# A mixture-of-experts stage on one Trainium2 core: W1 as the stationary operand, fetched for every tile of tokens

## The reference, cut to what matters

```python
def _L1_ffn_ref(x, router_W, router_b, ln_g, ln_b, W1, b1, W2, b2):
    B, S, H, E, K = (2, 512, 256, 8, 2)          # x here is 2 x 2048 x 256
    logits = x @ router_W + router_b
    w, idx = jax.lax.top_k(logits, K)
    w = jax.nn.softmax(w, axis=-1)
    gates = jnp.einsum('bske,bsk->bse', jax.nn.one_hot(idx, E, dtype=x.dtype), w)
    ...
    h = xhat[:, :, None, :] * ln_g + ln_b        # xhat: x, normalized
    a = jax.nn.gelu(jnp.einsum('bseh,ehf->bsef', h, W1) + b1, approximate=False)
    y = jnp.einsum('bsef,efh->bseh', a, W2) + b2
    y = y + x[:, :, None, :]
    out = jnp.einsum('bseh,bse->bsh', y, gates)
    return out
```

## Time and profile before

| | us |
|---|---|
| median of 3 runs | 4070.68 |
| lowest and highest | 4062.64, 4073.54 |
| the profiled execution, its own time | 4065.74 |
| its span in the trace | 4064.2 |
| PE busy in the span | 3197.6 (79%) |
| DVE busy | 2557.4 (63%) |
| ACT busy | 1755.8 (43%) |
| POOL busy | 1472.8 (36%) |

### The profile page before, as it was taken

How to read it: one execution, slowest core, us unless ns; L and a number is a source line. 1 busy time by engine, 2 the same in 40 slices (tenths; PEclk the granted TensorE clock), 3 DMA queues, 4 the chain that set the end, 5 groups by cost and what they waited for, 6 DMA issues and landing times. The chain is left out here.

```text
span 4064.2 us, 72075 instructions
## 1 busy us (share of the span) xinstructions
PE 3197.6 (79%) x21589; PEld 1637.2 (40%) x21590; DVE 2557.4 (63%) x6592; ACT 1755.8 (43%) x2093; POOL 1472.8 (36%) x811
## 2 busy tenths in 40 slices
PE   5539999999999989998335887788887339999970
PEld 2202333333333333332123454455565216666650
DVE  6739998989898989991476777354444302222226
ACT  3302887878787878889211222111211102222210
POOL 2212777777777777778100000000000230000016
PEclk8756999999999999999667999899997569999985
DMA  4743333333333333330230000110001550000014
GB/s 112 216 113 75 82 84 81 75 82 76 81 76 80 77 80 77 79 62 26 50 61 16 11 15 0 71 41 29 25 22 78 206 201 31 31 31 31 31 47 143
DMA packets 200466, 285.30 MB, mean 70 GB/s; under 512 B 91760, under 2 KB 156272, under 8 KB 197840
## 3 DMA queue, kind: packets, MB, share of 16 engines
q1 hardware_dynamic: 185968, 234.81, 23.0%
q0 software_dynamic: 13312, 43.30, 3.0%
q10 hardware_dynamic: 864, 3.15, 0.2%
HBM read 185.37 MB, written 79.00 MB: 65 GB/s over the span
## 5 line engine op out<-in xcount | busy, mean ns | idle before, releaser
L690 DVE CUSTOM_DVE_ANT_0 ps_r<-ps_r,toep 128x512 f32<-128x512 f32 x2048 | 1356.2, 717 | 194.8 <-PE ps_r L623 137.6
L779 ACT ACTIVATE prob<-ps_s,csc 128x1024 f32<-128x1024 f32 x768 | 836.7, 1119 | 185.1 <-PE ps_s L645 134.6
L623 PE MATMUL ps_r<-p 96*128 96x512 bf16 x2048 | 746.4, 403 | 130.9 <-DMA p<-scr_scratch 78.7
L737 POOL TENSOR_TENSOR tb<-tb,toep 128x1024 f32<-128x1024 f32 x256 | 606.1, 2367 | 484.7 <-ACT tb L769 336.6
L645 PE MATMUL ps_s<-p 120*128 120x512 bf16 (+1 forms) x2048 | 618.2, 384 | 41.9 <-ACT tb L769 26.6
L740 POOL TENSOR_TENSOR tb<-tb,mb 128x1024 f32<-128x1024 f32 x256 | 605.6, 2366 | 20.1
L661 PE MATMUL ps_o<-prob,vp 128*32 128x256 f32 x8192 | 553.1, 388 | 1.0 <-ACT prob L779 1.0
L623 PEld LDWEIGHTS ps_r<-p 96*128 96x128 bf16 x2048 | 199.1, 98 | 601.5 <-DVE mp L690 323.8
L769 ACT ACTIVATE tb<-ps_s 128x1024 f32<-128x1024 f32 x256 | 263.0, 1027 | 202.2 <-PE ps_s L645 202.1
L661 PEld LDWEIGHTS ps_o<-prob,vp 128*32 128x32 f32 x8192 | 214.8, 109 | 280.1 <-issue 190.7
L645 PEld LDWEIGHTS ps_s<-p 120*128 120x128 bf16 (+1 forms) x2048 | 181.6, 99 | 273.2 <-ACT prob L779 70.5
(11 more groups left out here) (289 smaller groups left out, 3540.2 us busy)
## 6 DMA issues: line engine op xcount, KB each, us to landing
p<-scr_scratch SPq DMA_DIRECT2D x288, 192.0 KB
mb<-mrow_scratch SPq DMA_DIRECT2D x16, 2048.0 KB, 7.1
scr_scratch<-part SPq DMA_DIRECT2D x64, 384.0 KB, 6.1
moe_w<-in_W_dram SPq DMA_DIRECT2D x16, 1024.0 KB
p<-scr_scratch SPq DMA_DIRECT2D x96, 128.0 KB
slots_scratch<-l_zero POOLq DMA_DIRECT2D x16, 592.0 KB, 5.2
e_xs<-slots_scratch SPq DMA_DIRECT2D x74, 128.0 KB, 2.0
yslots_scratch<-e_y SPq DMA_DIRECT2D x72, 128.0 KB, 1.7
```

What stands on the lines that cost most here:

```text
L623: pe.matmul(ps_r[:, bank, :], buf[:, hh, 0, qt * P:(qt + 1) * P], buf[:, hh, 1, kc * CH:(kc + 1) * CH], start=True, stop=True)\
L690: dve.tensor_tensor_reduce(ps_r[:, bank, :], ps_r[:, bank, :], toep[:, col:col + CH], 1.0, -3.0e38, ALU.mult, ALU.max, mp[:, whose.par, hh ...
L737: pool.tensor_tensor(tb[:, k % DIAGS], tb[:, k % DIAGS], toep[:, col:col + CH].unsqueeze(1) .broadcast_to([P, 2, CH]), ALU.mult).then_inc( ...
L779: act.activation(prob[:, n % RING], ps_s[:, mine % 2], ACT.Exp, scale=csc[:, qb * TB + kb:qb * TB + kb + 1]).then_inc(s["exp"], 1)
```

## The change

- The product of `up` is turned round. W1's 128 x 128 pieces are the stationary operand and `hT` (128 tokens) is the moving one: 16 products with 128 columns. The result has the hidden units on the partitions, which is the layout that `down` needs, so the 8 transposes, `ps_t` and ACT's copies are gone, and the gelu writes `aT` directly. `aT` has two buffers now.
- W1 isn't kept for all experts any more. SBUF holds it for two tiles; `stage_scatter` loads those of the first two, and in `stage_experts` SP's queue fetches the 1 MB of the tile after next once `up` of `this` has read its buffer. SP reads the expert from `owner` for that.
- Tokens: four buffers instead of two, loaded four tiles ahead. The loops have 18 passes with four tiles each.
- Results are stored from ACT's queue, behind the gelu of the next tile.
- b1, ln_g and ln_b are loaded as 96 rows of 128 and turned once by PE in `stage_scatter` into `cols`, a column for each row. The bias of a hidden unit is then a value per partition and piece, read with a stride of zero along the tokens. b2 and W2 stay as they were.
- The tables that go with it grow from 74 to 76 tiles (`AHEAD`), and two stages have more semaphores: 11 instead of 8, and 16 instead of 14.

The diff, cut:

```diff
-AHEAD = 2
+AHEAD = 4
+XS = 4
...
+COLS = E * (FK + 2 * KC)
...
 def stage_scatter(nc, g, a, w):
-        s = open_block(nc, ctx, "w load0 load1 put0 put1 ready eps passed", "s_")
+        s = open_block(nc, ctx, "w turn cols ident load0 load1 put0 put1 ready eps passed", "s_")
...
+        rows = sb("rows", [COLS, P])
...
+                sp.dma_start(rows[0:E * FK, :], a["b1"].rearrange("e (c p) -> (e c) p", p=P)).then_inc(s["w"], 16)
+                for i, n in enumerate(("ln_g", "ln_b")):
+                    at = E * FK + i * E * KC
+                    sp.dma_start(rows[at:at + E * KC, :], a[n].rearrange("e (c p) -> (e c) p", p=P)).then_inc(s["w"], 16)
+                for par in range(2):
+                    e = sp.value_load(g["owner"][0:1, par:par + 1], min_val=0, max_val=E - 1)
+                    sp.dma_start(w["w1"][:, par].unsqueeze(1), a["W1"][bass.ds(e, 1)].rearrange("a (c p) f -> p a c f", p=P))\
+                      .then_inc(s["w"], 16)
                 for e in range(E):
-                    sp.dma_start(w["w1"][:, e], a["W1"][e].rearrange("(c p) f -> p c f", p=P)).then_inc(s["w"], 16)
                     sp.dma_start(w["w2"][:, e], a["W2"][e].rearrange("(c p) n -> p c n", p=P)).then_inc(s["w"], 16)
-                    for n in ("ln_g", "ln_b"):
-                        sp.dma_start(w[n][:, e], a[n][e].rearrange("(c p) -> p c", p=P),
-                                     allow_slow_non_contiguous=True).then_inc(s["w"], 16)
...
+                    sp.dma_start(w["b2"][:, e], a["b2"][e].partition_broadcast(P)).then_inc(s["w"], 16)
...
+            @block.tensor
+            def _(pe):
+                pe.wait_ge(s["w"], up_to(16 * (5 + 2 * E)))
+                pe.transpose(ps_c[:, 0:COLS], rows[:], g["ident"][0:COLS, 0:COLS]).then_inc(s["turn"], 1)
...
 def stage_experts(nc, g, a, w):
...
-        xs = sb("xs", [P, 2, D])
+        xs = sb("xs", [P, XS, D])
...
-        u = sb("u", [P, 2, FF])
-        h = sb("h", [P, 2, FF])
-        aT = sb("aT", [P, FK, P])
+        u = sb("u", [P, 2, FK, P])
+        aT = sb("aT", [P, 2, FK, P])
...
             def _(sp):
...
                 def body(this, one, two):
-                    load(two)
-                    hold(sp, s["y"], this.times(1, 1), s["passed"])
-                    sp.dma_start(g["yslots"][bass.ds(this.times(P), P), :], y[:, this.par]).then_inc(s[f"store{this.par}"], 16)
+                    e = expert(sp, two)
+
+                    hold(sp, s["up"], this.times(1, 1), s["passed"])
+                    fetch(Tile(this.n, this.c + XS))
+                    sp.dma_start(w1[:, this.par].unsqueeze(1), a["W1"][bass.ds(e, 1)].rearrange("a (c p) f -> p a c f", p=P))\
+                      .then_inc(s[f"wfill{this.par}"], 16)
...
                 def up(tile):
-                    e = expert(pe, tile)
                     pe.wait_ge(s["affine"], up_to(tile.times(KC, KC)))
+                    if not isinstance(tile.n, int):
+                        pe.wait_ge(s[f"wfill{tile.par}"], up_to(tile.half(16)))
...
-                    for kc in range(KC):
-                        for half in range(2):
-                            mm = pe.matmul(ps_u[:, tile.par, half * CH:(half + 1) * CH], hT[:, kc, :],
-                                           w["w1"][:, bass.ds(e, 1), kc, half * CH:(half + 1) * CH]
...
+                    for f in range(FK):
+                        for kc in range(KC):
+                            mm = pe.matmul(ps_u[:, tile.par, f, :], w1[:, tile.par, kc, f * P:(f + 1) * P], hT[:, kc, :],
+                                           start=(kc == 0), stop=(kc == KC - 1), skip_group_check=True)
...
                 def body(this, one, two):
                     up(one)
-                    for half in range(2):
-                        if half == 0:
-                            pe.wait_ge(s["act"], up_to(this.times(1, UP0 + 1)))
-
-                        pe.wait_ge(s["trev"], up_to(this.times(2, half - 1 + FREE0)))
-                        for j in range(HALF):
-                            f = half * HALF + j
-                            mm = pe.transpose(ps_t[:, half, j * P:(j + 1) * P], h[:, this.par, f * P:(f + 1) * P], ident[:])
-                        mm.then_inc(s["tr"], 1)
                     turn(two)
                     e = expert(pe, this)
                     pe.wait_ge(s["y"], up_to(this.times(1)))
+                    pe.wait_ge(s["act"], up_to(this.times(1, UP0 + 1)))
...
             @block.scalar
...
-                    act.wait_ge(s["tr"], up_to(tile.times(2, FREE0 - 2)))
-                    act.activation(h[:, tile.par], u[:, tile.par], ACT.Gelu).then_inc(s["act"], 1)
+                    act.wait_ge(s["down"], up_to(tile.times(1, UP0 - 1)))
+                    act.activation(aT[:, tile.par], u[:, tile.par], ACT.Gelu).then_inc(s["act"], 1)
...
                     gelu(one)
+                    hold(act, s["y"], this.times(1, 1), s["passed"])
+                    act.dma_start(g["yslots"][bass.ds(this.times(P), P), :], y[:, this.par]).then_inc(s[f"kept{this.par}"], 16)
...
-                    dve.tensor_tensor(u[:, tile.par], ps_u[:, tile.par], of(w["b1"], e), ALU.add).then_inc(s["biased"], 1)
+                    dve.tensor_tensor(u[:, tile.par], ps_u[:, tile.par], of(b1, e).unsqueeze(2).broadcast_to([P, FK, P]),
+                                      ALU.add).then_inc(s["biased"], 1)
```

More of the change, by code:

```diff
@@ L1936, in walk @@
             start()
-            with eng.Fori(0, SLOT_TILES // 2) as n:
-                for c in range(2):
+            with eng.Fori(0, SLOT_TILES // XS) as n:
+                for c in range(XS):
                     body(Tile(n, c), Tile(n, c + 1), Tile(n, c + 2))
@@ L1943, in _ @@
             def _(pool):
[L1944 to L1947, removed]
+                pool.memset(aT[0:1, 0, 0, 0:1], 0.0).then_inc(s["biased"], UP0)
+                pool.memset(aT[0:1, 0, 0, 1:2], 0.0).then_inc(s["act"], UP0)
+                pool.memset(aT[0:1, 0, 0, 2:3], 0.0).then_inc(s["down"], UP0)
         with nc.Block() as block:
@@ L1951, in _, with fetch @@
             def _(sp):
[L1952 to L1956, removed]
+                def fetch(tile):
+                    sp.dma_start(xs[:, tile.c % XS], g["slots"][bass.ds(tile.times(P), P), :])\
+                      .then_inc(s[f"fetched{tile.c % XS}"], 16)
                 def body(this, one, two):
-                    load(two)
-                    hold(sp, s["y"], this.times(1, 1), s["passed"])
-                    sp.dma_start(g["yslots"][bass.ds(this.times(P), P), :], y[:, this.par]).then_inc(s[f"store{this.par}"], 16)
-                walk(sp, lambda: [load(Tile(0, c)) for c in range(2)], body)
+                    e = expert(sp, two)
[3 more added lines that the diff above has]
+                      .then_inc(s[f"wfill{this.par}"], 16)
+                walk(sp, lambda: [fetch(Tile(0, c)) for c in range(XS)], body)
                 for par in range(2):
-                    sp.wait_ge(s[f"store{par}"], up_to(16 * SLOT_TILES // 2))
-                    sp.wait_ge(s[f"load{par}"], 16 * (SLOT_TILES // 2 + 1))
+                    sp.wait_ge(s[f"wfill{par}"], up_to(16 * (SLOT_TILES // 2)))
+                for i in range(XS):
+                    sp.wait_ge(s[f"fetched{i}"], up_to(16 * (SLOT_TILES // XS + 1)))
             @block.tensor
@@ L1970, in turn @@
                 def turn(tile):
-                    pe.wait_ge(s[f"load{tile.par}"], tile.half(16) + 16)
+                    pe.wait_ge(s[f"fetched{tile.c % XS}"], up_to(tile.quarter(16, 16)))
                     if not (isinstance(tile.n, int) and tile.c == 0):
@@ L2069, in body @@
                     e = expert(dve, this)
-                    dve.wait_ge(s["down"], up_to(this.times(1, 1)))
-                    dve.wait_ge(s[f"store{this.par}"], up_to(this.half(16)))
+                    dve.wait_ge(s["down"], up_to(this.times(1, UP0 + 1)))
+                    dve.wait_ge(s[f"kept{this.par}"], up_to(this.half(16)))
                     dve.tensor_tensor(y[:, this.par], ps_d[:, 0:D], of(w["b2"], e), ALU.add).then_inc(s["y"], 1)
```

52 lines of the change are left out of this document (27 added, 25 removed).

## The result

The changed kernel took 3976.42 us (median of 4 runs, 3971.41 to 3985.89), the kernel before 4072.11 (median of 4, 4062.64 to 4084.4). The ratio is 0.9766, with a 95% interval from 0.9734 to 0.9798: 95.7 us less. 3978 had been forecast, in a range from 3963 to 4012. The interval of the ratio is 26 us wide, so that the two medians lie only 2 us apart is partly luck; what can be held against the forecast term by term is the profile.

A forecast was written before the change was run, and what follows sets the result against it. PE was taken to bound the experts' stage and POOL's transfers the scatter. From the 4070.68 us median, 91.7 us for 72 shorter tiles and 1.0 in the scatter gave 3978 us, range 3963 to 4012.

The forecast's parts named there:

- PE bounds the stage: Experts' stage: PE, busy 486.13 of 500 us at clock 1.00, sets the pace of 8.464 us a tile.
- The 91.7 us: Experts' stage: saving over 72 tiles, each 1.274 us shorter, 7.19 instead of 8.464.
- The bounds for a weight load: Up's 32 instructions: 0.111 us each was forecast, with bounds 0.1075 (up 3.44 us) and 0.125 (up 4.00 us).
- The step that failed: the tokens: Experts' stage: loading tokens four tiles early wins nothing beyond the wait before down; the old load landed just ahead of turn.
- the wait's 0.2 to 0.3: PE's wait for ACT's copy before down, 0.33 us in one tile and 0.20 in another, forecast to go with the copy.
- put this read at nothing: Ahead of down: PE's sequencer reads the expert's number while products queued before run, so it costs no time.
- The fetch: Experts' stage: W1's 1 MB lands in 4.4 to 5.5 us with 9.6 available, so it is hidden and costs nothing.
- the formula given: Rival of W1 landing late: a tile takes (3.55 + 1.2 + L) / 2, L from issue to landing; 4434 us, 3 in 100.
- The scatter: Scatter stage: -1.5 us from fewer waits for DMA engines, +0.5 for five more semaphores to clear, together -1.0.
- Weight loads that don't overlap: Rival in up: each load adds 0.108 us to 0.1075 of columns; tile 10.54 us, kernel 4220 us, 4 in 100.
- The sequencer wasn't late: Rival: a late sequencer leaves about half a microsecond's wait before down or up; 7.75 us a tile, 4018 us, 6 in 100.
- the clock stood at 1.00: Rival in the experts' stage: the granted clock falls to 0.95; 7.57 us a tile, 4006 us, 6 in 100.

The follow-up runs named there:

- the read off the ring: The changed kernel with tokens loaded two tiles ahead, stores by SP, and SP reading W1's expert behind the token load: 4053.09 us, ratio 0.9960 to the kernel before.
- no fetch, two, three: The changed kernel without W1's fetch in the loop (7.226 us a tile), with two fetches a tile (3968.18 us), or with three (4053.19 us).
- tokens late: The changed kernel with tokens loaded two tiles ahead and results stored by SP, as before: 4092.58 us, ratio 1.0059 to the kernel before.

## Why the prediction was right, and where it wasn't

**PE bounds the stage, and the tile is 3.55 + 0.22 + 3.42 = 7.19.** It is 3.57 + 0.22 + 3.45 = 7.24, or 7.251 over the whole stage. The 91.7 us were 88.4: 0.02 us too little for up and 0.03 for down, 72 times, is 3.6 us and about all of it. The bounds for a weight load (0.1075 and 0.125) held; it is 3.57 / 32 = 0.1116. Taken apart by the runs, each number being us a tile in the middle, in this order: 8.477 before; 8.385 with tokens early; 7.983 with the wait for the copy gone too; 7.108 without the transposes (and with W1 fetched); 7.245 with the product turned. So 0.09 + 0.40 + 0.88 - 0.14 = 1.23, and 72 times that is 88.7 us. The transposes were put at 0.87 and the turned product at 0.11. In another order the first two terms come out differently, since either alone gives about 0.1.

**The step that failed: the tokens.** The prediction said of loading them four tiles ahead that "nothing is won that the wait's 0.2 to 0.3 doesn't already hold", and named PE as what bounds the stage. Both were half true. The row it quoted, a load that lands "just ahead of turn", was no sign of slack. Behind the landing at 3604.66 came at once the read of the expert on PE's sequencer, and down had to wait for that. The prediction put this read at nothing "since no wait stops it"; this holds in the changed kernel only because its tokens are early. So the load was one side of a ring. Its parts at their mean are 2.03 to land, 0.94 to down where nothing else holds it, 3.92 to y, 0.66 to the store and 0.82 to the next load: 8.37 us, as long as PE's own chain with the wait for the copy, 8.385. Before, the two held down in turns, and the ring's load was issued 8.41 and 8.60 us after the one before. Taking the tokens out alone gains little for that reason (0.09 us a tile, 0.035 of it by the ring). Had the change left the load alone, the ring would have eaten five sixths of the gain (4053.09 us) or, with the read of the expert on it as well, all of it and more (4092.58). The total came out right because the change removes both, and the sum counted what PE does and never asked who else has this period. As far as this step goes that is luck: without the edit that the prediction put at nothing, five sixths of the gain would have been missing. For the same reason the wait before down doesn't simply go with ACT's copy: without the copy and with the ring, down started just as late.

**The fetch.** Forecast 4.4 to 5.5 us to land with 9.6 allowed; 5.2 measured, 7.5 did no harm, 11.0 did, by the formula given.

**The scatter.** -1.5 and +0.5 were forecast; -2.0 and +0.3 measured (the last transfer to the next stage's first write: 9.84 us before, 10.11 after). The third chunk waits 2.09 us, where it was 2.50. The drain is what it was, 5.3 us.

**The rivals.** Weight loads that don't overlap would have given 10.54 us a tile. The changed kernel has 0.1116 us an instruction with 128 columns, and 0.110 with 64; without overlap the second 64 columns alone would add 0.054. That settles it: they overlap nearly in full, though both use all rows. It is against the Trainium skill's rule in "TensorE: Matmul & The Clock Gate", Part 3, "The mechanism", as the prediction gives it; the same section excepts a load into a background weight buffer, which would fit, and no run here shows which it is. The sequencer wasn't late and the clock stood at 1.00.

## What to carry to other kernels

Before a busy engine is taken for the bound, look for a ring with the same period: a transfer that is issued behind the result of the tile before and lands "just in time" is one. Follow it through its parts (issue, landing, the work until the result, the store, the next issue), each at the shortest time that the trace shows for it. The plain distance from one load to the next is always one tile and proves nothing; but if the parts at their shortest come near the tile's time, a faster engine gains little until the load is taken out of the ring, by more buffers or another queue: here 16 us instead of 96. And of two waits that end together, removing either shows next to nothing (here 0.1 us a tile each, and 0.5 together): test them together before writing one off.

## What the runs showed of the hardware that was not expected

- For float32 with 128 x 128 weights, 64 moving columns cost almost what 128 do: 0.110 us an instruction against 0.1116.
- Transfers of 1 MB a tile beside PE's work, up to 326 GB/s, didn't change PE's pace at all: 7.245 us a tile in the middle without them, with one and with two.
- The first ups of a stage are no measure of a change. With the same work, after PE's long idle time at half clock, the first two took 6.79 and 5.46 us (changed kernel) or 6.58 and 5.46 (the read off the ring) in some profiles, and 5.22 to 5.63 and 3.83 in others (no fetch, two, three, tokens late), against 3.73 later. In the changed kernel's the granted clock rose at 3334.0 us, was back at half from 3337.4 to 3340.8, and then stayed at full.
- Eleven products of 512 columns had the clock at 1.00, and after them it fell to 0.50 within 4 us of idle time (from 3309.1 to 3312.7), before the barrier was through.
